# A GNN chain on one core: 3 of 16 gathered tiles a group become 0/1-matrix products in one attention pass, a second of 13 in layer 0; flag scatters by tile; edge counts spread over four passes

## The reference, cut to what matters

```python
# layer 0
msg = relu(x[src] + edge_attr @ We + be)
h = x + segment_sum(msg, dst)
layer0 = gelu(h @ W1 + b1) @ W2 + b2
# layer 1: four attention passes a, b, c, d; relu(batchnorm) after a and c
h = (x @ W).reshape(n, 8, C)
s_src, s_dst = (h * a_src).sum(-1), (h * a_dst).sum(-1)
e = leaky_relu(s_src[src] + s_dst[dst], 0.2)
ex = exp(e - segment_max(e, dst)[dst])
alpha = ex / segment_sum(ex, dst)[dst]
out = segment_sum(h[src] * alpha, dst)       # a, c: 8 heads side by side; b, d: their mean
# layer 2: five GRU steps
for _ in range(5):
    h_all = einsum('nd,ted->nte', h, W) + b              # 4 edge types
    a = segment_sum(h_all[src, edge_type_4], dst)
    h = gru_cell(a, h)
# layer 3
transformed = einsum('nd,rdo->nro', h, weight)           # 16 relations
layer3 = relu(segment_sum(transformed[src, edge_type_16] * edge_weight1, dst))
```

## Time and profile before

| what | value |
|---|---|
| median of 3 runs | 8553.75 us (8551.48 to 8554.43) |
| the profiled execution | 8555.38 us, span 8553.9 us, granted clock 0.789 |
| TensorE busy | 5386.7 us (63%) |
| VectorE busy | 4171.4 us (49%) |
| ScalarE busy | 2226.9 us (26%) |
| GpSimd busy | 5547.1 us (65%), 5774 instructions |
| the chain that ended last | TensorE 36%, GpSimd 29%, issue 16%, VectorE 12%, DMA 5% |

### The profile page before, as it was taken

One profiled execution on the slowest core, in us unless ns is written; L12 is line 12 of the kernel. 1 busy time (PEld: TensorE's weight loads), 2 busy tenths in 40 slices (PEclk: granted clock), 3 DMA queues, 4 the chain that ended last, 5 costly groups with the idle time before them and its releaser, 6 DMA issues.

```text
span 8553.9 us, 114467 instructions
## 1 busy us (share of the span) xinstructions
PE 5386.7 (63%) x41103; PEld 4896.7 (57%) x41103; DVE 4171.4 (49%) x8605; ACT 2226.9 (26%) x5853; POOL 5547.1 (65%) x5774
## 2 busy tenths in 40 slices
PE   4776625454466666445546688888899999933333
PEld 2554424444366665444444688877599999823322
DVE  8888534443444444466665556555422222233333
ACT  0000013333134343133332355555111111121111
POOL 7777677777777777777777777777760000067776
PEclk8888667777588887577776899999599999966666
DMA  6665432222144442233331666665298888721111
GB/s 211 228 236 178 45 59 64 62 63 61 40 115 116 115 115 71 75 121 113 112 121 48 175 183 181 181 182 148 77 363 329 330 329 329 274 65 27 27 27 27
DMA packets 438987, 1202.24 MB, mean 141 GB/s; under 512 B 160833, under 2 KB 234434, under 8 KB 397778
## 3 DMA queue, kind: packets, MB, share of 16 engines
q1 hardware_dynamic: 203188, 707.03, 23.6%
q0 software_dynamic: 235232, 487.88, 21.5%
HBM read 1071.01 MB, written 120.95 MB: 139 GB/s over the span
## 4 chain that ended last, share of the span: by engine, by line
PE 36%; POOL 29%; issue 16%; DVE 12%; DMA 5%; DVEq 1%; ACT 1%; SPq 0%; ACTq 0%; POOLq 0%
POOL pool L1415 24%; PE ps L1388 13%; PE ps L2052 12%; DVE ACC L471 3%; PE ps L505 3%; POOL ACC L486 2%; DMA pool<-d_h,srcT_s 2%; PE ps L1665 2%; DVE ACC L339 2%; DVE pool L494 1%; POOL edge_d L1194 1%; DMA pool<-b_h,srcT_s 1%; PE ps L1653 1%; POOL pool L486 1%; DVEq L454 1%
## 5 line engine op out<-in xcount | busy, mean ns | idle before, releaser
L1388 PE MATMUL ps<-pool 128*106 128x128 f32 (+2 forms) x19344 | 2543.1, 299 | 15.8 <-DVE pool L1288 15.8
L1388 PEld LDWEIGHTS ps<-pool 128*106 128x106 f32 (+2 forms) x19344 | 2515.4, 182 | 20.6 <-DVE pool L1288 18.4
L1346 ACT ACTIVATE ACC<-ps 72x256 f32 (+1 forms) x2418 | 1012.4, 419 | 1991.8 <-PE ps L1388 1748.6
L486 POOL DMA_INDIRECT ACC<-t,ACC x416 | 393.2, 945 | 1251.8 <-DVE ps L1929 1125.3
L1367 PE MATMUL ps<-ident,pool 128*128 128x128 f32 (+1 forms) x204 | 87.1, 427 | 1663.4 <-DVE pool L1246 1663.4
L1367 PEld LDWEIGHTS ps<-ident,pool 128*128 128x128 f32 (+1 forms) x204 | 35.7, 175 | 1702.3 <-issue 1702.3
L872 POOL DMA_INDIRECT cnt_d<-pool x806 | 826.3, 1025 | 281.8 <-issue 239.9
L1415 POOL DMA_INDIRECT pool<-a_h,srcT_s x806 | 778.1, 965 | 245.5 <-issue 244.3
L1415 POOL DMA_INDIRECT pool<-d_h,srcT_s x806 | 768.3, 953 | 245.6 <-issue 186.8
L1288 DVE TENSOR_TENSOR pool<-pool,ps 128x1024 f32<-128x1024 f32 (+1 forms) x807 | 927.5, 1209 | 0.0
L1415 POOL DMA_INDIRECT pool<-b_h,srcT_s x806 | 765.2, 949 | 245.7 <-issue 230.4
(11 more groups left out here) (325 smaller groups left out, 7078.0 us busy)
## 6 DMA issues: line engine op xcount, KB each, us to landing
ACC<-cnt_d SPq DMA_DIRECT2D x172, 1600.0 KB, 8.9
pool<-cnt_d SPq DMA_DIRECT2D x88, 1600.0 KB
cnt_d<-pool SPq DMA_DIRECT2D x26, 3200.0 KB
ACC<-key_d SPq DMA_DIRECT2D x31, 1792.0 KB, 8.7
ACC<-key_d SPq DMA_DIRECT2D x25, 2048.0 KB, 8.0
pool<-seg_d SPq DMA_DIRECT2D x100, 129.0 KB
cnt_d<-pool POOLq DMA_INDIRECT x806
pool<-a_h,srcT_s POOLq DMA_INDIRECT x806
```

Of the source, the lines that this page charges most:

```text
L486: g.indirect_dma_start(out=gb[b][:, k, :], out_offset=None, in_=table, in_offset=bass.IndirectOffsetOnAxis(ap=idx[:, c:c + 1], axis=0)).th ...
L1346: a.activation(win[:, 0:NPL, bass.ds(reg, 128)], pl[0].rearrange("p (i c) -> p i c", c=128), ACT.Copy).then_inc(*(tile_out if last else A) ...
L1388: mm = t.matmul(o, gbr[:, tile % RT, M * i:M * i + M], oh, start=True, stop=True)
```

## The change

Layer 0: `PG` becomes 2, so groups 6 to 61 gather 11 tiles of 13, and the second 0/1 matrix gets a buffer of its own; each is now made in one compare. One count instruction a group is left, with its 1.0 in SBUF (`onec`).

Pass c: from group 4 to 49 the last 3 of 16 tiles are products of the same kind. VectorE makes the three 0/1 matrices of group gi + 3 at the end of iteration gi, the j-th behind product j of the group in front. TensorE does the products of gi + 2 after tiles 1, 6 and 11 (25 matmuls each, 96 rows x 128 columns, x in three bf16 parts), ScalarE copies each result to SBUF, TensorE multiplies it with W and the score vectors (after tiles 4, 9 and 13), and ScalarE puts the row into the ring. An operand table is made before the pass. For C = 16 the PSUM sets become (2, 4).

Counts: 62 tiles in layer 0, 102 in pass a, 478 in b, 164 in c. `scatter_counts` waits for each of these parts before its first tile. `EARLY` 25 becomes 61, `LATE_D` 183 becomes 303; so in pass d 7 scatters stand between gathers, after it follow the same 16, 48 and 62, and then 303 late ones. Compared keys give FP16 hits.

Flags: 7 scatters by tile at group 5 of layer 0 in place of 25 by node; two loads of whole rows (halves) inside pass a in place of two of single elements before it; the scan in two halves in groups 2 and 6.

The sizes of the program and the inputs are otherwise the same, but for one more small input (`dstL`, the destination of the edge ahead of each tile).

```diff
-PG, FIRST = 1, 6
+PG, FIRST = 2, 6
+Q_A, Q_B = 31, 82
...
-        def vector_multiplicity(gi):
-            p = gi // 2
-            if gi % 2 == 0:
-                v.wait_ge(krow_in[p % 2].sem, 16 * (p // 2 + 1))
-            v.wait_ge(*V.now())
-            for c in range(gi * K + gi * K % 2, (gi + 1) * K, 2):
...
+        COUNTED = {"l0": (0, Q_A, (0, 2)), "a": (Q_A, Q_B - Q_A, (0, 2)), "b": (Q_B, NQ - Q_B, (0, 1, 2, 3)), "c": (0, Q_B, (1, 3))}
+        def quads_of(name, gi):
+            q0, n, _ = COUNTED[name]
+            return range(q0 + n * gi // NGR, q0 + n * (gi + 1) // NGR)
+        def vector_tile_counts(name, q, row, which, unit):
+            hits = count_hits[name].bitcast(FP16).rearrange("p (j c) -> p j c", c=512)
+            v.wait_ge(*V.now())
+            for j, k in enumerate(which):
+                c = 4 * q + k
+                if c < NT:
+                    count = v.scalar_tensor_tensor(out=hits[:, j, :], in0=row, scalar=keyT[:, c:c + 1],
+                                                   in1=unit.to_broadcast([128, 512]), op0=ALU.is_equal, op1=ALU.mult,
+                                                   accum_out=cmul[:, c:c + 1])
+            count.then_inc(*V.one())
+        def vector_counts_done(name):
+            v.tensor_copy(cval[:, c0:c1:by], cmul[:, c0:c1:by]).then_inc(*counts_ready.one())
+        def vector_counts_l0(gi):
+            q = gi // 2
+            if gi % 2 == 0:
+                v.wait_ge(rows_in[q % 2].sem, 16 * (q // 2 + 1))
+            vector_tile_counts("l0", q, count_rows["l0"][q % 2], (gi % 2 * 2,), onec[:, 0:1])
...
+        def gpsimd_tile_flags():
+            g.wait_ge(*flag0.now())
+            g.wait_ge(*mark["tile_flags"])
+            for j in range(7):
+                g.indirect_dma_start(
+                    out=flag_d, out_offset=bass.IndirectOffsetOnAxis(ap=tile_slot[:, j:j + 1], axis=0),
+                    in_=tile_flag[:, j, :], in_offset=None).then_inc(*flagged.one())
...
-                for b0, n, x in nodes:
-                    made = v.tensor_tensor(out=hotT[j][:, b0:b0 + n, :],
-                                           in0=src_row[:, j, :].unsqueeze(1).to_broadcast([128, n, 128]),
-                                           in1=x, op=ALU.is_equal)
+                v.tensor_tensor(out=hotT[j], in0=src_row[:, j, :].unsqueeze(1).to_broadcast([128, NB, 128]), in1=nodes,
+                                op=ALU.is_equal).then_inc(*hot_made.one())
...
-        EARLY, TAIL_, BESIDE, MERGED, AFTER = 25, 16, 48, NS, 8
+        EARLY, TAIL_, BESIDE, MERGED, AFTER = 61, 16, 48, NS, 8
-        BESIDE_D, MERGED_D, LATE_D, CHUNK = 48, 2 * NS, 183, 8
+        BESIDE_D, MERGED_D, LATE_D, CHUNK = 48, 2 * NS, 303, 8
...
                 if i == NT // 2:
                     g.wait_ge(*counted.now())
-                    g.wait_ge(*odd_ready.now())
+                if i in (0, 2 * Q_A, 2 * Q_B, NT // 2):
+                    g.wait_ge(counts_ready.sem, (0, 2 * Q_A, 2 * Q_B, NT // 2).index(i) + 1)
...
-            s.dma_start(frs, flag_d[0:SPL, 0:1].rearrange("s o -> o s")).then_inc(*flag_in.one())
-            s.dma_start(grs, flag_d[0:SPL, 1:2].rearrange("s o -> o s")).then_inc(*flag_in.one())
+        def sync_slot_flags(h):
+            s.wait_ge(*flagged.now())
+            s.dma_start(flags, flag_d[HSL * h:HSL * h + HSL, :].rearrange("s k -> (s k)").unsqueeze(0)).then_inc(*flag_in.one())
...
+        BY_PRODUCTS, FIRST_G = {"c": 3}, 4
+        PICK, PICK_COPY, ROW, ROW_PUT = (1, 6, 11), (1, 7, 11), (4, 9, 13), (5, 9, 13)
...
-            S, R = {16: (4, 3), 32: (2, 3), 64: (1, 3)}[C]
+            S, R = {16: (2, 4), 32: (2, 3), 64: (1, 3)}[C]
...
+            def vector_hots(u):
+                for j in range(PP):
+                    v.wait_ge(src_rows.sem, sr0 + u - FIRST_G + 1)
+                    if u > FIRST_G:
+                        v.wait_ge(picked_mm.sem, pm0 + product_no(u - 1, j) + 1)
+                    v.tensor_tensor(out=hotT[j], in0=src_row[:, j, :].unsqueeze(1).to_broadcast([128, NB, 128]), in1=nodes,
+                                    op=ALU.is_equal).then_inc(*hots_made.one())
+            def tensor_pick(u, j):
+                n = product_no(u, j)
+                t.wait_ge(hots_made.sem, hm0 + n + 1)
+                if n:
+                    t.wait_ge(rows_put.sem, rp0 + n)
+                for b in range(NB):
+                    mm = t.matmul(pick_out, x3[:, b, :, :].rearrange("p k f -> p (k f)"), hotT[j][:, b, :], start=(b == 0),
+                                  stop=(b == NB - 1))
+                mm.then_inc(*picked_mm.one())
+            def scalar_pick(u, j):
+                a.wait_ge(picked_mm.sem, pm0 + product_no(u, j) + 1)
+                a.activation(picks, pick_out, ACT.Copy).then_inc(*picked.one())
+            def tensor_row_product(u, j):
+                t.wait_ge(picked.sem, pc0 + product_no(u, j) + 1)
+                t.matmul(row_out, picks, wst, start=True, stop=True).then_inc(*row_mm_.one())
...
+                    if layer < 3:
+                        vector_counts(name, gi, r0)
+                    if by_products(gi + 3):
+                        vector_hots(gi + 3)
...
-                    for c in range(c0, c0 + n):
+                    for c in range(c0, c0 + n - by_products(gi)):
```

More of the change, by code:

```diff
@@ L311, in vector_keys @@
             mark["cidx"] = V.now()
+            v.tensor_tensor(out=tile_slot, in0=dst0[:, :], in1=tile_no, op=ALU.add).then_inc(*V.one())
+            v.tensor_scalar(tile_flag[:, :, 0], tile_no, 0.0, None, ALU.is_equal).then_inc(*V.one())
+            v.tensor_tensor(out=tile_flag[:, :, 1], in0=dst0[:, :], in1=dst_before, op=ALU.not_equal).then_inc(*V.one())
+            mark["tile_flags"] = V.now()
         def sync_keys():
@@ new lines, in sync_count_rows_l0 @@
+        def sync_count_rows_l0(gi):
+            q = gi // 2
+            if gi == 0:
+                s.wait_ge(*key_out.now())
+                s.wait_ge(*flag0.now())
+                s.wait_ge(*mark["cidx"])
+            if gi % 2 == 0:
+                if q >= 2:
+                    s.wait_ge(*mark["counts", "l0", 2 * q - 3])
+                row = key_rows[512 * q:512 * q + 512]
+                s.dma_start(count_rows["l0"][q % 2], row.partition_broadcast(128)).then_inc(*rows_in[q % 2].one())
+                if q < NS2:
+                    s.dma_start(cnt4[q][:, 0:2 * HALF * 128].rearrange("p (r c) -> p r c", r=8),
+                                zero.unsqueeze(1).to_broadcast([128, 8, 1600])).then_inc(*filled.one())
@@ L885, in gpsimd_late_counts, with gpsimd_first_counts @@
             g.memset(tick[:, CHUNKS_D:CHUNKS_D + 1], 0.0).then_inc(*late_done.one())
-        def gpsimd_flags():
-            g.wait_ge(*flag0.now())
-            g.wait_ge(*mark["fslot"])
-            for b in range(NB):
-                g.indirect_dma_start(
-                    out=flag_d, out_offset=bass.IndirectOffsetOnAxis(ap=node[:, b:b + 1], axis=0),
-                    in_=fpair[:, b, :], in_offset=None).then_inc(*flagged.one())
-            g.wait_ge(*counted_ready.now())
+        def gpsimd_first_counts():
             g.wait_ge(*filled.now())
@@ L1012, in vector_odd_counts @@
-        def vector_odd_counts(gi):
-            j, (c0, n) = gi // 2, GR[gi]
-            if gi % 2 == 0:
-                v.wait_ge(odd_in[j % 2].sem, 16 * (j // 2 + 1))
-            v.wait_ge(*V.now())
-            for c in range(c0 + 1, c0 + n, 2):
-                q = c // 4 * 4 - KT * j
-                row = odd_row[j % 2][:, 128 * q:128 * q + 512]
-                hits = row if c % 4 == 3 else spare1[c // 4 % 4]
-                count = v.scalar_tensor_tensor(out=hits, in0=row, scalar=odd_key[:, c:c + 1], in1=odd_unit.to_broadcast([128, 512]),
-                                               op0=ALU.is_equal, op1=ALU.mult, accum_out=odd_mul[:, c // 2:c // 2 + 1])
-            count.then_inc(*V.one())
-            mark["odd", j] = V.now()
+        count_unit = ps[7][:, 256:257]
@@ new lines, in pair_quads, with sync_count_rows, vector_counts @@
+        def pair_quads(name, p):
+            return range(quads_of(name, 2 * p)[0], quads_of(name, min(2 * p + 1, NGR - 1))[-1] + 1)
+        def sync_count_rows(name, p):
+            if p >= 2:
+                s.wait_ge(*mark["counts", name, 2 * p - 3])
+            q = pair_quads(name, p)
+            s.dma_start(count_rows[name][p % 2][:, 0:512 * len(q)],
+                        key_rows[512 * q[0]:512 * (q[-1] + 1)].partition_broadcast(128)).then_inc(*rows_in[p % 2].one())
+        def vector_counts(name, gi, r0):
+            p = gi // 2
+            if gi % 2 == 0:
+                v.wait_ge(rows_in[p % 2].sem, r0[p % 2] + 16 * (p // 2 + 1))
+            for q in quads_of(name, gi):
+                k = 512 * (q - pair_quads(name, p)[0])
+                vector_tile_counts(name, q, count_rows[name][p % 2][:, k:k + 512], COUNTED[name][2], count_unit)
+            mark["counts", name, gi] = V.now()
```

(8 more changed lines are left out.)

251 lines of the change are left out of this document (146 added, 105 removed).

## The result

The changed kernel takes 8445.6 us (median of 4 runs, 8443.6 to 8447.31), the kernel before 8552.6 in the same comparison: ratio 0.9875, 95% interval 0.986 to 0.989. The forecast was 8418 in a range of 8310 to 8525. The profiled execution took 8447.06 us at a span of 8445.8; against the span before (8553.9) it is 108.1 us less, where the sum said 136.

A forecast was written before the change was run, and what follows sets the result against it. GpSimd's instructions at 1.25 to 1.33 us each were taken to bound layer 0 and the passes. The terms -43 -34 -3 +9 +14 +2 -20 -205 +144 = -136 gave 8418 us, range 8310 to 8525.

The forecast's parts named there:

- Layer 0: Layer 0: 56 fewer gathers save 70 us, seven flag scatters cost 9 and SBUF contention 18: -43 us (-61 to -20).
- The +18 for the second SBUF input: Layer 0: 62 compares with two SBUF inputs slow the gathers beside them by 0.29 us each: +18 us (0 to 31).
- Table a: End of layer 0 and table a: GpSimd's 61 counts start at 958.9, first gather near 1078.3 instead of 1112.6: -34 us.
- Pass a: Pass a: the slot map's add is gone, its scans are halved but not fewer elements: -3 us.
- Between the passes: Stretches after passes a and b: tail scatters wait for VectorE's last counts: +9 and +14 us (together +10 to +30).
- Pass c: Pass c: 138 gathers go, but a chain across engines binds at 19.6 us a group: -20 us (-69 to +23).
- the chain leaves idle gaps of about 3 us, so I take the full level of 2.4 GHz: Pass c: TensorE's clock stays at its full level despite the idle gaps; the period of 19.6 us assumes this.
- the clock's: Rival, pass c: one longer gap a group leaves TensorE at 1.2 GHz, period 27.8 us, +359 us, 8797; chance 0.08.
- The product at 82 ns a matmul: Rival, pass c: product matmuls take 82 ns each instead of 70, pass c +23 us, 8461 in all; chance 0.18.
- Pass d and step 0 of the GRU stage: Pass d loses 156 scatters, GpSimd still binding: -205 us; 120 of them, now late, delay step 0: +144 us.
- late counts stay hidden: Rival, step 0 of the GRU stage: the late count scatters cost nothing, the 144 us vanish, 8274 in all; chance 0.05.
- d is bound by its chain: Rival, pass d: TensorE and VectorE bind at 22 us a group instead of GpSimd: +97 us, 8515; chance 0.08.

The follow-up runs named there:

- the edit that takes the second one away: The changed kernel with three edits, one spreading VectorE's counts of pass b over 48 groups: 8217.8 us, with b to c 190.8 us against 209.9.
- the run that undid it: The changed kernel with 120 of its 303 late scatters put into pass c: 8280.5 us; in another run back between pass d's gathers: 8462.2 us.

## Why the prediction was right, and where a term was off

The sum was off by 28 us of 136: the table of a is 12 of them, pass c 22 and the stretch behind it 7, and passes a and d with step 0 give 12 back.

*What bounds it.* Right: passes a, b and d and layer 0 run at one GpSimd instruction per 1.25 us before and after, and removing instructions there paid what the count says. In d, the period of 20.1 us was forecast and measured (mean of 50 distances of the score copy 20.10).

*Layer 0*, -43 forecast, -44.1 measured. The +18 for the second SBUF input was taken from twelve occurrences of another instruction; undoing it alone gave 17.9 back. The Trainium skill's "GPSIMD Engine Reference", section "8. Key points", names two SBUF inputs of a VectorE instruction as one of two things that contend with GpSimd; the rows of the counts, the scan and the subtraction agree.

*Table a*, -34 forecast, -22.0 measured: the one term whose own rule I had and did not apply. The 61 counts were put at 1.275 us each, though they now lie beside VectorE's scan and subtraction at the end of layer 0, where before GpSimd had been idle:

```profile
917.83 1.00 POOL L897 DMA_INDIRECT cnt_d<-pool  x1 [2.98 <-DVE pool L358]
...
926.79 6.36 POOL L897 DMA_INDIRECT cnt_d<-pool  x1 [0.31 <-issue]
933.45 3.28 POOL L897 DMA_INDIRECT cnt_d<-pool  x1 [0.30 <-issue]
```

5.4 and 2.3 us over the usual, and 2.98 of waiting for the last counts of layer 0, make 10.7 of the 12.

*Pass a*, -3 forecast, -7.4 measured: the same rule, not applied here either. Before the change three gathers of this pass lay beside long VectorE instructions of the slot map, beside its scan, its add (4.99 us for the gather) and a product with a constant:

```profile
1218.88 8.60 DVE L967 TENSOR_TENSOR_SCAN ACC<-onec,ACC 1x4064 f32<-1x4064 f32 x1
1219.08 9.16 POOL L1415 DMA_INDIRECT pool<-a_h,srcT_s  x1 [0.30 <-issue]
...
1311.22 2.26 DVE L976 TENSOR_SCALAR ACC<-ACC 1x4064 f32<-1x4064 f32 x1
1311.33 2.96 POOL L1415 DMA_INDIRECT pool<-a_h,srcT_s  x1 [0.31 <-issue]
```

The gathers over 1.02 us were 15.7 us above the usual 0.945 before and are 9.2 above it after (5.40 and 5.46 beside the two half scans), which is 6.5 of the 7.4. The third instruction has one input in SBUF only, and the gather beside it is long all the same; so two SBUF inputs are not the only case.

*Between the passes*, +9 and +14 (and 2 for the table) forecast, +8.1 and +18.9 measured: right, and shown by the edit that takes the second one away.

*Pass c*, -20 forecast, +2.4 measured, and 6.7 more in the stretch behind it, as this stretch begins with the last gather and the chain lags behind the gathers. The step that failed is "the chain leaves idle gaps of about 3 us, so I take the full level of 2.4 GHz". It rested on a gap of 3.28 us after which one turn still took 0.30, against one of 4.73 with 0.45. Two rows could not carry it, and the trace before already had the rows that say so: in the same pass d the length of the gap does not tell the level, as with these two:

```profile
5477.90 0.44 PE L1367 MATMUL ps<-ident,pool 128*128 128x128 f32 x1 [3.58 <-DVE pool L1246]
5502.21 0.30 PE L1367 MATMUL ps<-ident,pool 128*128 128x128 f32 x1 [3.58 <-DVE pool L1246]
```

After the change 3.2 us of idling a group came with a low clock in nearly every group of c. What hid the error is luck, a second one of the other sign: at the upper level the chain is 17.47 us long, not 19.6. The product was taken at 1.75 us and takes 1.40; three of them are 1.05 less. TensorE's waits for ScalarE were put at 2.4 and are 0.89 and 0.35, 1.16 less. Together 2.2, where 2.1 are missing. So at the upper level pass c would have gained 2.5 us a group, 115 us (with the gap filled it is 877.6 us, 130 less than before the change), and the clock took 3.0 a group back. Had the chain been as long as forecast, the same 3.0 us would have cost 46 x 3.0 = 138 us against the forecast and made 8556 us (an estimate): outside the stated range, and no gain at all. Of the rivals, the clock's had the right mechanism and a wrong size: its 27.8 us let the clock be low for the whole group (twice both terms, as its words say, would even be 30.4), but only about the first 6 us after the gap run at the lower level. The product at 82 ns a matmul is out (56 ns): the 81 ns that the Trainium skill gives for a sustained stream of such pairs ("TensorE: Matmul & The Clock Gate", "Back-to-back issue gap") are not what these rows show.

*Pass d and step 0 of the GRU stage*, -205 and +144 forecast, -209.3 and +140.4 measured, and each alone by the run that undid it. The late scatters' marks after the change:

```profile
L908 POOL MEMSET pool<- x37: 88/88/89, 5915.5 to 6285.8; 1x1 f32 x37
```

37 marks, 10.3 us apart as the 22 before; the cover was used up as said. That late counts stay hidden, and that d is bound by its chain, are out.

## What to carry to other kernels

Where several engines hand a group round, look for the one instruction that stands in front of a hand-over and is needed by nobody yet: here one compare of 1.8 us, moved behind one hand-over on its engine, was worth 170 us, some 125 of them by the clock, where the swap of 138 gathers for products had brought none. Keep TensorE's gaps short in such a chain, or fill them: the gap costs itself once and the clock after it a second time. Read many gaps of the trace, not one, before you rely on the clock. And where GpSimd issues DMAs beside long VectorE instructions with two operands in SBUF, try one of them in PSUM.

## What the runs showed of the hardware that I had not expected

The same chain can run at 17.5 or at 20.5 us a group: on the chip of the later runs the changed kernel starts the products of pass c at the first and is at the second some eight groups later; in its first run it is near the second from the start. What tips it over is not settled by these runs. The length of the single gap is not it: 3.07 to 3.12 us ended at either level, and so did 3.58 us in pass d of the kernel before.

The kernel before took 18% longer on another chip (10134.5 us), where the profiles of its variants show waits that nothing in them releases, and the order of the versions changed: there the kernel with products in c (with the counts of b moved) was at 1.0221 of the kernel before (1.0196 to 1.0246), on the first chip the changed kernel is at 0.9875. Where the standstills come from, no row says.
